# Every second PSUM eviction of the transposed attention weights moves from VectorE to ScalarE

## What is computed

```python
xn  = layernorm(x)
# attention: 16 heads of 64, rotary, causal
q, k = rotary(xn @ Wq.T), rotary(xn @ Wk.T);  v = xn @ Wv.T
scores = einsum('bhqd,bhkd->bhqk', q, k) * 64 ** -0.5     # masked above the diagonal
attn   = softmax(scores)
a      = einsum('bhqk,bhkd->bhqd', attn, v) -> (b, t, 1024) @ Wo.T
# experts: 8, top 2 by gate, computed densely
f      = sum_e gate[e] * (silu(xn @ W1[e].T) * (xn @ W2[e].T)) @ W3[e].T
out    = x + a + f
```

## Time and profile before

| | |
|---|---|
| median of the runs shown | 6374.08 us (2 runs: 6003.2 and 6744.95) |
| profiled execution, its own time | 6004.29 us |
| its span, slowest core (core 4) | 6002.7 us |
| spans of the 8 cores | 5995.7 to 6002.7 us |
| granted TensorE clock, mean of a core | 0.87 |
| TensorE, VectorE, ScalarE busy | 4985.1, 2624.3, 991.9 us |

### The profile page before, as it was taken

One profiled execution on the slowest core, in us unless ns is written; L12 is line 12 of the kernel. 1 busy time (PEld: TensorE's weight loads), 2 busy tenths in 40 slices (PEclk: granted clock), 3 DMA queues, 4 the chain that ended last, 5 costly groups with the idle time before them and its releaser, 6 DMA issues.

```text
span 6002.7 us, 73838 instructions; the slowest of 8 cores (5995.7 to 6002.7 us)
## 1 busy us (share of the span) xinstructions
PE 4985.1 (83%) x24512; PEld 2453.8 (41%) x24880; DVE 2624.3 (44%) x5268; ACT 991.9 (17%) x2017; POOL 281.3 (5%) x536
## 2 busy tenths in 40 slices
PE   2355666666666569999999999999999999999998
PEld 2333333333333334444444444444444444444444
DVE  2346666656666633333333333333333333333333
ACT  2222222222222211011011011011010010110110
POOL 0000000000000000000000000000000000000000
PEclk9985665665665569999999999999999999999999
DMA  2000000000000002222222222222222222222222
GB/s 45 22 16 1 10 10 1 10 10 1 10 10 1 3 11 38 40 36 40 38 37 39 38 38 38 38 37 40 41 37 36 43 39 33 39 40 37 38 41 79
DMA packets 81898, 173.82 MB, mean 29 GB/s; under 512 B 9336, under 2 KB 9592, under 8 KB 81536
## 3 DMA queue, kind: packets, MB, share of 16 engines
q0 software_dynamic: 76496, 152.13, 17.1%
q1 hardware_dynamic: 5040, 16.94, 0.8%
HBM read 312.74 MB, written 8.39 MB: 53 GB/s over the span
## 4 chain that ended last, share of the span: by engine, by line
PE 77%; DVE 14%; issue 5%; ACT 3%; DMA 1%; DVEq 1%; ACTq 0%; SPq 0%; POOLq 0%
PE pp L574 20%; PE pp L584 20%; PE pp L619 20%; DVE stat L464 5%; DVE poolb L418 4%; PE pp L427 4%; PE pp L345 4%; PE pp L456 3%; PE pp L409 1%; PE pp L527 1%; PE pp L387 1%; PE pp L259 1%; DVE stat L469 1%; ACT poolb L482 1%; ACT poolb L488 1%
## 5 line engine op out<-in xcount | busy, mean ns | idle before, releaser
L574 PE MATMUL pp<-xn,poolb 128*128 128x512 bf16 x5526 | 1331.6, 381 | 5.6
L584 PE MATMUL pp<-xn,poolb 128*128 128x512 bf16 x5513 | 1324.2, 380 | 6.3
L619 PE MATMUL pp<-poolb 128*128 128x512 bf16 x5519 | 1212.1, 379 | 6.0
L598 DVE TENSOR_TENSOR arf<-pp,arf 128x512 f32<-128x512 f32 x704 | 487.1, 692 | 1442.0 <-PE pp L584 1442.0
L594 ACT ACTIVATE arf<-pp 128x512 f32<-128x512 f32 x704 | 420.3, 597 | 2618.9 <-PE pp L574 2618.8
L574 PEld LDWEIGHTS pp<-xn,poolb 128*128 128x128 bf16 x5632 | 552.6, 98 | 671.3 <-issue 13.1
L584 PEld LDWEIGHTS pp<-xn,poolb 128*128 128x128 bf16 x5632 | 552.5, 98 | 670.0 <-issue 9.5
L619 PEld LDWEIGHTS pp<-poolb 128*128 128x128 bf16 x5632 | 551.2, 98 | 664.4
L629 DVE TENSOR_TENSOR acc<-acc,pp 128x512 f32<-128x512 f32 x512 | 352.1, 688 | 850.7 <-PE pp L619 833.8
L409 PE MATMUL pp<-dgb,poolb 128*128 128x128 bf16 x2176 | 306.6, 305 | 342.0 <-DVE poolb L418 268.7
L427 PE MATMUL pp<-poolb 128*64 128x128 bf16 x2176 | 277.6, 310 | 323.8 <-DVE poolb L418 314.7
(11 more groups left out here) (82 smaller groups left out, 1672.5 us busy)
## 6 DMA issues: line engine op xcount, KB each, us to landing
poolb<-w_l POOLq DMA_DIRECT2D x352, 256.0 KB, 4.6
poolb<-w_l POOLq DMA_DIRECT2D x128, 352.0 KB, 4.4
arf<-x SPq DMA_DIRECT2D x16, 512.0 KB, 3.5
out<-arf SPq DMA_DIRECT2D x16, 512.0 KB, 2.7
poolb<-wq_l POOLq DMA_DIRECT2D x8, 256.0 KB, 4.1
poolb<-wqs_l POOLq DMA_DIRECT2D x8, 256.0 KB, 5.3
poolb<-wk_l POOLq DMA_DIRECT2D x8, 256.0 KB, 5.7
poolb<-wks_l POOLq DMA_DIRECT2D x8, 256.0 KB, 5.7
```

The source lines that it names most:

```text
L574: em("tensor", [(lambda cc, tt, bk, kkc, fi, la: lambda e: e.matmul(pps(BK(bk)), pb[:, W1B[cc % 2] + kkc * 128:W1B[cc % 2] + (kkc + 1) * 128],
L584: em("tensor", [(lambda cc, tt, bk, kkc, fi, la: lambda e: e.matmul(pps(BK(bk)), pb[:, W2B[cc % 2] + kkc * 128:W2B[cc % 2] + (kkc + 1) * 128],
L598: em("vector", (lambda bk, tbb, ebb, tt: lambda e: e.tensor_tensor(arfs(H2S[tbb], 512), pps(BK(bk)), arfs(WBC[ebb] + tt * 512, 512), ALU.m ...
L619: em("tensor", [(lambda mm, tt, bk, cll, fi, la: lambda e: e.matmul(pps(BK(bk)), pb[:, W3B[mm % 2] + cll * 128:W3B[mm % 2] + (cll + 1) * 128],
```

## The change

In the second stage, the copy of a group from PSUM to `ATT` is emitted for ScalarE when g is even and for VectorE, as before, when g is odd. The place of the call in the program, the banks, the sizes and the result type are the same; `copy` is ScalarE's form of `tensor_copy`.

```diff
@@ -415,11 +415,18 @@
-                    em("vector", (lambda gg, bk, n: lambda e: e.tensor_copy(
-                        pb[:, ATT + gg * 512:ATT + gg * 512 + n * 128],
-                        pp[:, BK(bk)[0]:BK(bk)[0] + n * 128]))(g, bank, kbn),
-                       reads=[("pp",) + BK(bank)],
-                       writes=[("pb", ATT + kb0 * 128, ATT + (kb0 + kbn) * 128)])
+                    if g % 2 == 0:
+                        em("scalar", (lambda gg, bk, n: lambda e: e.copy(
+                            pb[:, ATT + gg * 512:ATT + gg * 512 + n * 128],
+                            pp[:, BK(bk)[0]:BK(bk)[0] + n * 128]))(g, bank, kbn),
+                           reads=[("pp",) + BK(bank)],
+                           writes=[("pb", ATT + kb0 * 128, ATT + (kb0 + kbn) * 128)])
+                    else:
+                        em("vector", (lambda gg, bk, n: lambda e: e.tensor_copy(
+                            pb[:, ATT + gg * 512:ATT + gg * 512 + n * 128],
+                            pp[:, BK(bk)[0]:BK(bk)[0] + n * 128]))(g, bank, kbn),
+                           reads=[("pp",) + BK(bank)],
+                           writes=[("pb", ATT + kb0 * 128, ATT + (kb0 + kbn) * 128)])
```

## The result

| | span of the profiled execution, us | time against before |
|---|---|---|
| before | 6002.7 | |
| changed | 6357.7 | 1.058 [1.056, 1.060] |

The change costs 355 us, in a profiled execution of 6359.4 us. The prediction said 6352 for such an execution. The median over all 11 runs of the changed kernel is 6459 us (6357 to 7058), since in six of them the cores of one die or both had a lower mean granted clock. That median lies outside the predicted range of 6260 to 6430. Before has a median of 6006 us over 10 runs (6003 to 6745). The spans further down are those of the profiled executions.

What follows compares the result with a forecast made beforehand. The score loop was taken as bound by a chain of handovers, no engine being full. Late copies summed to 43.5 us per head pair, 348 over eight; added to 6004 this gave 6352 us, range 6260 to 6430.

Steps and rivals of the forecast that it cites:

- The circle over X: Score loop: from L476's start (X) over last copy, L427, L456, L464 to next X; late copies lengthen it, 348 us.
- The queue's order: ScalarE, score loop: moved copies stand behind L482 and L488, starting 0.58 us after L482's end; none can pass an Exp.
- The waits: TensorE, score loops: L427 and L409 would wait mostly for copies, together growing from 583 to over 900 us.
- The terms: Loss per head pair by unit size: one group 5.4 us, two 8.8, three 15.0, four 14.5.
- the handover to TensorE: From a copy's end to TensorE's start in the score loop: 0.14 to 0.15 us from VectorE or ScalarE.
- 237 us that VectorE loses: VectorE's busy time would fall by about 237 us through the 48 of 80 copies moved per head pair.
- After the loop: The eighth four-group second stage of a pair has no Exp ahead and gains some 0.2 us.
- The range: Whole kernel: 6260 to 6430 us, from errors of 0.35 us a unit down and 0.3 up; about 8 in 10.
- Side by side: Rival, score loop: ScalarE's copy starts when Exp now starts, parallel to VectorE's; 33 us gained, 5971 us; chance 0.04.
- VectorE's load: Rival, score loop: VectorE's work is the bound, so all 237 us come off, 5767 us; chance 0.03.
- small units hide the delay: Rival: VectorE's L501 to L512 hold L464 in one- and two-group units; only long classes pay, 234 us, 6239; chance 0.07.
- Handovers that cost more: Rival: each ScalarE step in the circle costs another 0.35 us, 130 us on top, 6482 us; chance 0.04.

Runs made afterwards that it cites:

- The late reciprocal: VectorE's L501, L509, L512 emitted behind the next unit's first row maximum, against the kernel with all copies on ScalarE ahead of Exp (5837 us): 5882.7 us.
- the first experiment: Against the changed kernel, even copies go to ScalarE only in second stages of one or two groups: 6120.3 us, ratio 1.021.
- the last experiment: Against the changed kernel, TensorE's wait for ScalarE's semaphore placed last among an operation's waits instead of first: 6378.0 us, ratio 1.064.

## Why the prediction was right and wrong

**What bounds the kernel: right.** The circle over X, the last copy, L427, L456 and L464 gave the loss to 7 us (348 predicted, 355 measured), and their direction to the first six of the eight experiments. The late reciprocal went the second of the two ways named. The order of the waits did what was expected inside the loops, at half the size.

**The queue's order: right.** ScalarE is free 0.58 us after the end of L482 by the earlier trace rows; 893.38 - 890.93 - 1.86 = 0.59. Moving nothing but the order turned 355 us of loss into 134 of gain. The Trainium skill (PSUM — Partial Sum Buffer, Engine vs sequencer instructions) has ScalarE's queue strictly first in, first out; the traces here agree with it, in none of the rows read does a copy pass an Exp. The Trainium skill's rule on parallel reads of PSUM (same page, Specifications (TRN2)) also holds where VectorE copies from 890.76 on and Exp reads from 890.93 on in other banks, each in its usual time (0.68 and 1.86 us). It says nothing of when a read may start.

**The waits: right, with a trap in the names.** The waits of L409 and L427 for copies, 583 us before, were to grow to over 900. They are 1012 us now, if the waits of L434 that stand under L516 (234.6), L508 (31.9) and L425 (7.5) are counted as what they are, waits for copies. The list of waits has only a part of L434's time under ScalarE (us in total, times, longest us):

```profile
PE pp L409 <- ACT poolb L419: 524.4, 128, 5.1
...
PE pp L434 <- DVE stat L516: 234.6, 80, 3.9
PE pp L434 <- ACT poolb L419: 213.5, 128, 3.2
```

L434 does not need L516, a reciprocal for the next second stage. It waits for VectorE's copy, long over, and for ScalarE's. In unit (7, 0):

```profile
748.97 0.56 ACT L419 CAST poolb<-pp 128x512 bf16<-128x512 f32 x1
...
749.43 0.16 DVE L516 RECIPROCAL stat<-stat 128x1 f32<-128x1 f32 x1
...
749.78 0.93 PE L434 MATMUL pp<-poolb 128*64 128x128 bf16 x7 [3.52 <-DVE stat L516]
```

L516 ran just then, and the view names the last event of an engine that is waited for. The code tells which instruction it can be.

**The terms: nearly right.** In the pair read, one-group and four-group units came within 0.3 us of 5.4 and 14.5. Two and three groups took 0.8 and 1.0 more, and the step that was mis-sized is "the handover to TensorE is 0.14 to 0.15 us from either engine". It was read where only one engine was waited for. Where L434 waits for both, ScalarE first by name, and ScalarE ends last, it takes 0.25: 748.97 + 0.56 = 749.53 to 749.78. Eight units of 0.11 are 0.9 in each class, and the last experiment takes 0.8 away in each. That is up to 14 us too little over the eight pairs. A part of it was made up by one-group units (0.2 a pair less than predicted) and by what follows the loop (0.4 a pair more gained), so that the total of 348 is nearer than its terms are. The prediction's 237 us that VectorE loses were 208: copies that follow each other overlap (two of 683 ns take 1.28 us in the earlier trace rows) and the sum counts the overlap twice. Nothing hung on it.

**After the loop: right, but for the clock.** The eighth second stage of four groups was to gain 0.2 us. In five of the eight pairs it gained 0.16 to 0.17. In the other three, the pair of the table among them, it is 1.2 to 1.4: from the last L427 of the table to the next pair's L345 it took 7.72 us before (815.46 to 823.18), and 6.40 from L434 after (907.23 to 913.63). The 16 matmuls at the end account for 0.83 of it, 1.05 instead of 1.88 us, at a clock that rose sooner (last section). The prediction had no term for that.

**The range: wrong.** It was worked out for an execution like the profiled one, with 0.35 us down and 0.3 up for each unit, and 6359 lies in it. The median of 6459 does not. The step that failed is the sentence that sets the sum against "the lower of the runs shown" and leaves the other, 6745 us, out. The runs showed a term of 100 us in its place, from the profiled execution's 6359 to the median, and of 700 us in the longest run. Neither the range nor the chances held such a term, and one of the two runs shown, 12% over the other, gave reason for one. How large it would be could not be read from two runs: over 10 runs the kernel before has a median of 6006, only 2 us above its profiled execution. How much of the changed kernel's 100 us is chance stays open.

**The rivals.** Side by side did not come by this change. Made true by the order of the queue, it brought 134 us and not the 33 of the rival's sum, since the copies then start well before X, which I had not thought of. VectorE's load is refuted by the kernels that free VectorE and are slower, and that small units hide the delay by the first experiment. Handovers that cost more are real, but by 0.11 us and not 0.35.

## What to carry to other kernels

Before work moves to an idle engine, look at what stands ahead of it in that engine's queue at that moment: ScalarE, 17% busy, was busy exactly when it was needed. In this kernel a copy that the inner circle waits for belongs ahead of the Exp that start no earlier than it is ready, and behind them it costs their whole length. A moved instruction pays only if it is ready before its turn, as the late reciprocal shows from the other side. And when a term is read from rows, its conditions are read with it: the handover of 0.15 us held where one engine was waited for.

## What the runs showed of the hardware that was not expected

- A second wait of TensorE that has long been fulfilled adds about 0.11 us when it stands behind the one that comes last: 0.25 against 0.14 us from the end of ScalarE's copy, and 0.25 against 0.15 from VectorE's with the order turned round.
- ScalarE's copies of 512 columns from PSUM follow each other at 0.47 to 0.48 us, though each is 0.56 to 0.59 long; behind an accumulator read a copy starts after 0.09 us, an Exp from SBUF after 0.29.
- At the end of a score loop TensorE's granted clock sometimes rose before the dense matmuls began. In the pair above the last 16 matmuls of the changed kernel took 1.05 us, the 2.4 GHz level, and the granted clock is 0.58 from 907 to 912 us and 1.00 from 912 to 914. In the first pair the same 16 took 1.89. In both, TensorE had stood idle for 0.45 and 0.94 us just ahead. On this core it came in three of the eight pairs of the changed kernel, on the others in three to six, never in the first or fourth. It does not come from the change: in the kernel before it came once on five of the eight cores, and with the copies of even groups ahead of Exp in four or five pairs of every core. What makes one pair differ from another was not found.

```profile
912.42 1.05 PE L434 MATMUL pp<-poolb 128*64 128x128 bf16 x16 [0.94 <-DVE poolb L425]
913.63 4.70 PE L345 MATMUL pp<-xn,poolb 128*128 128x512 bf16 x21 [0.16 <-issue]
```
